# Cross attention by scans and a gated FFN on one core: half gate slots, the weight check summed by TensorE, and residuals over three engines

## The chip, the cores and the metric

The kernel runs on one core of a Trainium2 chip. The metric is the device time of an execution in microseconds (us). The engines are TensorE (PE, with its weight loads as PEld), VectorE (DVE), ScalarE (ACT), GpSimd (POOL) and SyncE (SP), which issues most of the transfers.

## The reference, cut to what matters

Input x is [16, 128, 256], ctx (the values v) the same. One layer: an exponentially decaying average over the 128 time steps (the "wkv" recurrence) with keys layernorm(x), then a feed-forward part of 704 hidden channels.

```python
k = _layernorm(x)
# per channel, over t:   y_t = (sum_{s<t} e^{-(t-1-s)w + k_s} v_s + e^{u+k_t} v_t) / (the same without v)
x = x + wkv(time_decay, time_first, k, ctx_2048)
n = _layernorm(x)
g = einsum('th,ih->ti', n, gate_w) * gate_s
u = einsum('th,ih->ti', n, up_w) * up_s
x = x + einsum('ti,hi->th', silu(g) * u, down_w) * down_s
```

gate_w, up_w and down_w hold only -1, 0 and 1.

## The kernel before

**Tiling.** The 16 sequences are 8 units of two (`UB`), and two units are a group (`GU`) of 512 tokens (`GT`). The first part runs by unit `u`, the FFN by group `g`. The 704 hidden channels are five full tiles of 128 and a rest of 64, six tiles a group (`MC`), numbered on as `n = 6 g + m` (0 to 23).

**A unit's steps.** VectorE makes the statistics of x (`stats1`, `aggr1`), ScalarE the reciprocal deviation (`rstd1`), GpSimd the bias (`bias1`, for units from 2 on in pairs: u = 3, 5, 7), ScalarE the exponentials (`expk`). GpSimd multiplies v by them (`weigh`, units 0 to 3) or VectorE does (`mulp`, units 4 to 7). TensorE transposes both (`e_T`, `p_T`), VectorE runs the recurrences as scans (`scan_e`, `scan_p`) and combines them (`denom`, `numer`), ScalarE makes the reciprocal as log and exponential (`log_den`, `recip`), GpSimd multiplies (`divide`) and adds to x in the channel layout (`first`, `add_y`, buffer `xc`). Then TensorE transposes back (`x1_T`), VectorE makes statistics (`stats2`, `aggr2`), `rstd2` the factors, ScalarE normalises (`norm2`), TensorE transposes (`n_T`), and the result is split into a rounded part and a remainder: `high_n` on ScalarE (`xh`), `low_n` on VectorE (`xl`).

**A group's FFN.** `gate(n)` and `up(n)` are four matmuls of 512 columns each (two halves of the channels, xh and xl), into one of three PSUM slots (`ps_f`, `RING`), taken in turn. `silu(n)` on ScalarE reads the gate's slot, `gated(n)` on VectorE the up's slot and writes `h`. `high_h` (ScalarE) rounds h to `hh`, `low_h` (GpSimd) subtracts to `hl`, and `down(n)` accumulates four matmuls into `ps_d`. The rest tile n = 5, 11, 17, 23 has gate and up in one slot, and `low_rest` on VectorE in place of `low_h`. After six tiles `finish(g)` on VectorE scales `ps_d` and adds it to `xc` in two passes, and SyncE stores each pass. The last tiles of the last group are split into `down` and `downb` by output half.

**The weight check.** Weights come as float32, are copied to a rounded type by GpSimd (`whi`, four equal quarters of the gate and up weights in layout order, then two halves of the down weights). ScalarE sums the low halves of their words (`wcheck`), VectorE compares the three sums with 0 (`wany_`), TensorE adds over the partitions (`count`), VectorE copies the number to `flag` (`publish`), and TensorE reads it and branches to `rest_of_program`, on the rounded weights or the exact ones.

**Order.** Each engine's order is written out by hand in its block. `warm(k)` is k products of the identity with itself, into a slot not yet in use; there are 45 in the opening and 5 in `rest_of_program`. ScalarE switches table sets by `tables(...)`: the exponential and logarithm are in one, silu in another. SyncE's output loop goes by group and half:

```python
for g in range(GROUPS):
    for c in range(CC):
        sp.wait_ge(s_fin, CC * g + c + 1)
        sp.dma_start(out_ch[...], xc[:, c, ...]).then_inc(s_out, 16)
```

Of the kernel before, what the change touches and what calls it, by code (L numbers as in the profile page):

```python
# [5 lines left out]
ALU = mybir.AluOpType  # L6
# [7 lines left out]
P = 128  # L14
# [16 lines left out]
RING = 3  # L31
TAIL = 3 * MC + 2
# [20 lines left out]
def build(nc, x_tok, x_ch, v_tok, v_ch, w_gu, w_d, vecs, out_ch):  # L53
    with ExitStack() as ctx:
# [6 lines left out]
        def sem(name):  # L61
# [16 lines left out]
        mhalf = sb("mhalf", [P, UB])  # L78
# [9 lines left out]
        wany = sb("wany", [P, CC + 1])  # L88
# [31 lines left out]
        hx = sb("hx", [P, GT], F32R)  # L120

# [28 lines left out]
        s_gate, s_up, s_sil, s_h, s_hh, s_hl, s_hx, s_dn, s_fin = (sem(n) for n in (  # L150
            "s_gate", "s_up", "s_sil", "s_h", "s_hh", "s_hl", "s_hx", "s_dn", "s_fin"))
# [52 lines left out]
        def _(sp):  # L204
# [31 lines left out]
        def _(pool):  # L236
# [45 lines left out]
            def rstd2(u):  # L282
# [3 lines left out]
                else:  # L286
# [3 lines left out]
                    nc.gpsimd.tensor_tensor(rs2[:, seqs(u)], ve2[:, seqs(u)], mhalf[:, :], ALU.pow).then_inc(s_rs2, 1)  # L290
# [24 lines left out]

            bias1(0); weigh(0); bias1(1); bias1(3); weigh(1); divide(0); whi(0); first(0); add_y(0); divide(1)
            add_y(1); weigh(2); rstd2(0); whi(1); whi(2); rstd2(1); bias1(5); whi(4); weigh(3); whi(3); divide(2)
            first(1); add_y(2); whi(5); divide(3); rstd2(2); low_h(0); low_h(1); add_y(3); low_h(2); low_h(3)
            rstd2(3); bias1(7); first(2); divide(4); add_y(4); low_h(4); rstd2(4); divide(5); add_y(5); low_h(6)
            low_h(7); rstd2(5); low_h(8); low_h(9); first(3); divide(6); add_y(6); low_h(10); rstd2(6); divide(7)  # L320
            add_y(7); low_h(12); low_h(13); rstd2(7); low_h(14); low_h(15); low_h(16); low_h(18); low_h(19); low_h(20)
            low_h(21); low_h(22)

        @block.scalar
        def _(act):
# [17 lines left out]
            def rstd1(u):  # L343
# [6 lines left out]
                act.wait_ge(s_lv1, k)  # L350
# [72 lines left out]
            def high_h(n):  # L423
# [4 lines left out]
                if m < FULL:  # L428
                    nc.scalar.activation(hh[:, m, :], h[:, n % HS, :], ACT.Copy).then_inc(s_hh, 1)  # L429
                else:  # L430
                    nc.scalar.activation(hx[REST:P, :], h[REST:P, n % HS, :], ACT.Copy).then_inc(s_hh, 1)

            rstd1(0); elift_(); expk(0); rstd1(1); expk(1); rstd1(3); log_den(0); recip(0); expk(2); wcheck(0)
            wcheck(1); log_den(1); recip(1); wcheck(2); expk(3); log_den(2); rstd2a(0); rstd1(5); recip(2); rstd2a(1)
            norm2(0); norm2(1); high_n(0); expk(4); high_n(1); expk(5); log_den(3); recip(3); tables(SILU); silu(0)
            silu(1); high_h(0); silu(2); norm2(2); high_h(1); silu(3); high_h(2); high_n(2); high_h(3); silu(4)
            silu(5); tables(LN_EXP); log_den(4); rstd1(7); recip(4); norm2(3); expk(6); high_n(3); high_h(4)
            high_h(5); log_den(5); expk(7); recip(5); tables(SILU); silu(6); silu(7); norm2(4); high_h(6); silu(8)
            high_n(4); tables(LN_EXP); log_den(6); high_h(7); recip(6); tables(SILU); silu(9); high_h(8); norm2(5)
            high_h(9); silu(10); silu(11); high_n(5); high_h(10); tables(LN_EXP); log_den(7); high_h(11); recip(7)  # L440
            tables(SILU); silu(12); silu(13); norm2(6); high_h(12); high_n(6); silu(14); high_h(13); silu(15)
            high_h(14); silu(16); norm2(7); high_h(15); high_h(16); high_n(7); silu(17); silu(18); high_h(17)
            high_h(18); silu(19); silu(20); high_h(19); silu(21); high_h(20); high_h(21); silu(22); silu(23)
            high_h(22); high_h(23)

        @block.vector
        def _(dve):
# [22 lines left out]
            def wany_():  # L470
# [313 lines left out]
```

## Time and profile before

| | |
|---|---|
| time, median of 3 runs | 105.62 us (105.26 to 105.83) |
| profiled execution, its own time | 105.38 us |
| its span, first to last instruction | 103.6 us |
| busy: TensorE | 93.5 us (90%) |
| busy: VectorE | 80.9 us (78%) |
| busy: ScalarE | 78.1 us (75%) |
| busy: GpSimd | 67.4 us (65%) |
| HBM read, written | 8.55 MB, 2.10 MB |

Busy shares are averages over stages with different limits: the opening to about 28 us, the FFN with the later units beside it, the FFN alone from about 79 us, and the stores at the end. The mean granted TensorE clock was 0.98 of the full one.

### The profile page before, as it was taken

The page shows a single profiled execution, that of the slowest core. Times are in us where ns is not written, and L with a number is a line of the kernel's source. Part 1 is how long each engine was busy: PE and PEld are TensorE (multiplying, and loading weights), DVE is VectorE, ACT ScalarE, POOL GpSimd, SP SyncE. Part 2 cuts the span into 40 slices and gives each one's busy share as a digit, 9 for nine tenths or more (in the row PEclk, how much of TensorE's full clock was granted, in tenths as well). Part 3 has the DMA queues.
Part 4 walks back from the last instruction along what each step waited for, and adds up shares of the span by engine and source line. Part 5 has one row for each costly group of instructions (what it writes and reads, how often), then busy time and mean ns, then how long its engine had stood idle before and what let it go on. Part 6 is the DMA issues. An engine that isn't in the chain of part 4 may idle for free.

```text
span 103.6 us, 1646 instructions
## 1 busy us (share of the span) xinstructions
PE 93.5 (90%) x482; PEld 75.8 (73%) x482; DVE 80.9 (78%) x170; ACT 78.1 (75%) x136; POOL 67.4 (65%) x96
## 2 busy tenths in 40 slices
PE   3997988766999999999999999999999999999930
PEld 3987977644988888668788787858888888888610
DVE  1879999999998999999998998997843544543650
ACT  4355999989995799999999999997858443655400
POOL 2016686999986799894990889869888404364500
PEclk9999999997699999999999999999999999999998
DMA  2999999998000000000005000000500000500005
GB/s 43 301 364 380 406 360 375 377 376 310 23 0 0 0 3 6 0 0 0 0 0 203 0 0 0 9 0 0 203 0 0 0 0 3 193 16 0 0 27 188
DMA packets 6475, 10.78 MB, mean 104 GB/s; under 512 B 576, under 2 KB 3648, under 8 KB 6336
## 3 DMA queue, kind: packets, MB, share of 16 engines
q1 hardware_dynamic: 6320, 10.62, 28.8%
q8 instruction: 6, 0.10, 0.4%
q10 hardware_dynamic: 144, 0.03, 0.3%
q14 instruction: 5, 0.04, 0.1%
HBM read 8.55 MB, written 2.10 MB: 103 GB/s over the span
## 4 chain that ended last, share of the span: by engine, by line
PE 67%; DVE 13%; ACT 7%; DMA 4%; issue 3%; DVEq 1%; SPq 1%
PE ps_f L671 39%; PE ps_d L687 17%; DMA xt<-x_tok 4%; DVE sbe L506 3%; ACT nt L387 3%; PE ps_x L653 3%; PE ps_x L645 2%; DVE st L481 2%; DVE sbp L517 2%; PE ps_f L698 2%; DVE den L531 2%; PE ps_a L626 1%; PE ps_b L635 1%; ACT rden L372 1%; DVE num L541 1%
## 5 line engine op out<-in xcount | busy, mean ns | idle before, releaser
L671 PE MATMUL ps_f<-xh,wgu_r 128*128 128x512 f32 x88 | 36.1, 410 | 0.0
L313 POOL TENSOR_TENSOR hl<-h,hh 128x512 fp32r<-128x512 f32 x20 | 25.7, 1292 | 14.0 <-ACT hh L429 13.9
L671 PE MATMUL ps_f<-xl,wgu_r 128*128 128x512 f32 x88 | 34.8, 396 | 0.0
L578 DVE SCALAR_TENSOR_TENSOR h<-ps_f,vec,sil 128x512 f32<-128x512 f32 (+1 forms) x24 | 17.9, 747 | 11.4 <-PE ps_f L671 7.2
L671 PEld LDWEIGHTS ps_f<-xh,wgu_r 128*128 128x128 f32 x88 | 16.6, 188 | 4.6 <-ACT sil L418 0.7
L671 PEld LDWEIGHTS ps_f<-xl,wgu_r 128*128 128x128 f32 x88 | 16.6, 188 | 3.3
L418 ACT ACTIVATE sil<-ps_f,vec 128x512 f32<-128x512 f32 x20 | 13.5, 687 | 6.8 <-PE ps_f L671 6.7
L698 PE MATMUL ps_f<-ident 128*128 128x128 f32 x100 | 15.8, 320 | 1.6 <-POOL ident L241 1.6
L687 PE MATMUL ps_d<-hh,wd_r 128*128 128x512 f32 x40 | 16.3, 407 | 0.0
L698 PEld LDWEIGHTS ps_f<-ident 128*128 128x128 f32 x100 | 14.9, 234 | 1.6 <-POOL ident L241 1.6
L687 PE MATMUL ps_d<-hl,wd_r 128*128 128x512 f32 x40 | 15.8, 394 | 0.0
L429 ACT ACTIVATE hh<-h 128x512 fp32r<-128x512 f32 x20 | 12.6, 629 | 2.8 <-DVE h L578 2.8
L327 ACT ACT_TABLE_LOAD x8 | 10.3, 1283 | 1.3 <-PEq L778 1.2
L272 POOL TENSOR_TENSOR yk<-num,rden 128x508 f32<-128x508 f32 x8 | 10.3, 1282 | 1.4 <-ACT rden L372 0.8
L278 POOL TENSOR_TENSOR xc<-xc,yk 128x508 f32<-128x508 f32 x8 | 10.2, 1280 | 0.7
L517 DVE TENSOR_TENSOR_SCAN sbp<-decay,ps_b 128x512 f32<-128x512 f32 x8 | 9.7, 1213 | 0.1
L358 ACT ACTIVATE ek<-xt,nb,rs 128x256 f32<-128x256 f32 x16 | 8.7, 590 | 1.4 <-POOL nb L250 1.4
L506 DVE TENSOR_TENSOR_SCAN sbe<-decay,ps_a 128x512 f32<-128x512 f32 x8 | 9.6, 1204 | 0.0
L687 PEld LDWEIGHTS ps_d<-hh,wd_r 128*128 128x128 f32 x40 | 7.5, 188 | 2.1 <-POOL hl L313 0.4
L687 PEld LDWEIGHTS ps_d<-hl,wd_r 128*128 128x128 f32 x40 | 7.5, 188 | 1.6
L387 ACT ACTIVATE nt<-ps_x,nb,rs 128x256 f32<-128x256 f32 x14 | 7.1, 560 | 0.4 <-POOL nb L294 0.3
L531 DVE SCALAR_TENSOR_TENSOR den<-ps_a,fcol,sbe 128x254 f32<-128x254 f32 x16 | 6.9, 474 | 0.0
(73 smaller groups left out, 133.1 us busy)
## 6 DMA issues: line engine op xcount, KB each, us to landing
xt<-x_tok SPq DMA_DIRECT2D x8, 256.0 KB, 7.6
xc<-x_ch SPq DMA_DIRECT2D x4, 512.0 KB, 10.8
out_ch<-xc SPq DMA_DIRECT2D x8, 256.0 KB, 2.5
wgu<-w_gu SPq DMA_DIRECT2D x1, 1408.0 KB, 8.3
vc<-v_ch SPq DMA_DIRECT2D x2, 512.0 KB, 10.5
wd<-w_d SPq DMA_DIRECT2D x1, 768.0 KB, 9.7
vt<-v_tok SPq DMA_DIRECT2D x2, 256.0 KB, 4.9
vt<-v_tok SPq DMA_DIRECT2D x1, 512.0 KB, 11.4
```

The costliest lines, as they stand in the source:

```text
L272: nc.gpsimd.tensor_tensor(yk[:, u % 2, :, 1:T], num[:, u % 2, :, 1:T], rden[:, u % 2, :, 1:T], ALU.mult).then_inc(s_y, 1)
L313: nc.gpsimd.tensor_tensor(hl[:, m, :], h[:, n % HS, :], hh[:, m, :].bitcast(F32), ALU.subtract).then_inc(s_hl, 1)
L327: nc.scalar.preload_act_table_set(name)
L387: last = nc.scalar.activation(nt[:, u % 2, b, :], x1_bank(u)[:, b * C:(b + 1) * C], ACT.Identity, scale=rs2[:, q:q + 1], bias=nb2[:, q:q + 1])
L418: nc.scalar.activation(sil[:, n % 2, :], f, ACT.Silu, scale=vec[:, V_GS + m:V_GS + m + 1]).then_inc(s_sil, 1)
L429: nc.scalar.activation(hh[:, m, :], h[:, n % HS, :], ACT.Copy).then_inc(s_hh, 1)
L506: nc.vector.tensor_tensor_scan(sbe[:, u % 2, :, :].rearrange("p q t -> p (q t)"), decay[:, :, :].rearrange("p q t -> p (q t)"), ps_a[:, :, ...
L517: nc.vector.tensor_tensor_scan(sbp[:, u % 2, :, :].rearrange("p q t -> p (q t)"), decay[:, :, :].rearrange("p q t -> p (q t)"), ps_b[:, :, ...
L578: nc.vector.scalar_tensor_tensor(h[r, n % HS, :], ps_f[r, slot(n, 1) % RING, :], vec[r, V_US + m:V_US + m + 1], sil[r, n % 2, :], ALU.mult ...
L671: last = nc.tensor.matmul(ps_f[:, i % RING, :], w, a, start=c == 0 and x is xh, stop=c == CC - 1 and x is xl)
L687: last = nc.tensor.matmul(ps_d[:, c, :], wd_r[:, m, cs] if exact else wd[:, m, cs], a if exact else a.bitcast(F32), start=m == 0 and i == ...
L698: nc.tensor.matmul(ps_f[:, RING - 1, 0:P], ident[:, :], ident[:, :], start=True, stop=True)
```

## The change

1. **Half gate slots** (`HALVED = 3`): the first three products, gate(0), up(0) and gate(1), are each made in two halves of 256 columns: `gatea` and `upa` for unit 0, as soon as its xl is there (`s_xl` 1), and the other half for unit 1 later.
2. **Check**: `wany_` is gone; `count` sums the three sums themselves, and `publish` compares that number with 0.
3. **Weight copies by tile**: gate and up tiles are interleaved in memory, and `whi` copies three tiles at a time (`PIECE`); a product waits only for its own tiles, `down` for its half of the down weights.
4. **Two residuals elsewhere** (`FIN_ACT = (0, 1)`): for groups 0 and 1 ScalarE scales `ps_d` into a buffer (`settle`, two passes) and GpSimd adds it to `xc` (`add_res`, one instruction). SyncE waits for `s_res` there.
5. **No identity products.**
6. `high_h` of tiles 7, 10, 13 and the reciprocal deviations `rs1` for units 5 and 7 (with their pairs) go from ScalarE to GpSimd; the rest tile's gated value stays in its PSUM slot, which is free only after `low_rest`.
7. **New orders** on the four engines. ScalarE loads tables six times in place of eight.

The diff, cut:

```diff
+HALVED = 3
+PIECE = 3
+HIGH_POOL = (7, 10, 13)
+FIN_ACT = (0, 1)
+RSTD_POOL = (5, 7)
...
+            if k == 2 * FULL:
+                eng.wait_ge(s_hx, g + 1)
+            elif k % 2 == 0:
                 eng.wait_ge(s_sil, n + 1)
...
             for g in range(GROUPS):
                 for c in range(CC):
-                    sp.wait_ge(s_fin, CC * g + c + 1)
+                    if g in FIN_ACT:
+                        sp.wait_ge(s_res, FIN_ACT.index(g) + 1)
+                    else:
+                        sp.wait_ge(s_fin, CC * (g - len([i for i in FIN_ACT if i < g])) + c + 1)
...
+                if u in RSTD_POOL:
+                    i = RSTD_POOL.index(u) + 1
+                    pool.wait_ge(s_mv1, u + 1)
+                    nc.gpsimd.tensor_scalar(lv1[:, q], mv1[:, q, 1], 1.0, EPS, ALU.mult, ALU.add).then_inc(s_ve1, 1)
+                    pool.wait_ge(s_ve1, i)
+                    nc.gpsimd.tensor_tensor(rs1[:, q], lv1[:, q], mhalf[:, :], ALU.pow).then_inc(s_rs1p, 1)
+                    pool.wait_ge(s_rs1p, i)
...
+            def high_h(n):
+                g, m = divmod(n, MC)
+                pool.wait_ge(s_h, n + 1)
+                if g >= 1:
+                    pool.wait_ge(s_dn, CC * (n - MC + 1))
+                nc.gpsimd.tensor_copy(hh[:, m, :], h[:, n % HS, :]).then_inc(s_hhp, 1)
+
+            def add_res(g):
+
+                pool.wait_ge(s_x1, GU * (g + 1))
+                pool.wait_ge(s_set, CC * (FIN_ACT.index(g) + 1))
+                ts = slice(g * GT, (g + 1) * GT)
+                nc.gpsimd.tensor_tensor(xc[:, :, ts], xc[:, :, ts], dsc[:, FIN_ACT.index(g) % 2, :, :], ALU.add).then_inc(s_res, 1)
...
-            bias1(0); weigh(0); bias1(1); bias1(3); weigh(1); divide(0); whi(0); first(0); add_y(0); divide(1)
-            add_y(1); weigh(2); rstd2(0); whi(1); whi(2); rstd2(1); bias1(5); whi(4); weigh(3); whi(3); divide(2)
-            first(1); add_y(2); whi(5); divide(3); rstd2(2); low_h(0); low_h(1); add_y(3); low_h(2); low_h(3)
-            rstd2(3); bias1(7); first(2); divide(4); add_y(4); low_h(4); rstd2(4); divide(5); add_y(5); low_h(6)
-            low_h(7); rstd2(5); low_h(8); low_h(9); first(3); divide(6); add_y(6); low_h(10); rstd2(6); divide(7)
-            add_y(7); low_h(12); low_h(13); rstd2(7); low_h(14); low_h(15); low_h(16); low_h(18); low_h(19); low_h(20)
-            low_h(21); low_h(22)
+            bias1(0); weigh(0); bias1(1); bias1(3); weigh(1); whi(0); divide(0); whi(1); first(0); add_y(0); divide(1)
+            add_y(1); weigh(2); rstd2(0); first(1); weigh(3); rstd2(1); bias1(5); divide(2); add_y(2); whi(2); whi(4)
+            whi(5); whi(3); rstd2(2); divide(3); add_y(3); first(2); low_h(0); low_h(1); low_h(2); low_h(3); rstd2(3)
+            bias1(7); low_h(4); first(3); divide(4); add_y(4); divide(5); rstd2(4); add_y(5); high_h(7); low_h(6)
+            low_h(7); low_h(8); low_h(9); rstd2(5); high_h(10); low_h(10); divide(6); add_y(6); rstd2(6); divide(7)
+            high_h(13); add_y(7); low_h(12); low_h(13); rstd2(7); low_h(14); low_h(15); low_h(16); add_res(0)
+            low_h(18); low_h(19); low_h(20); low_h(21); low_h(22); add_res(1)
...
+            def settle(g):
+
+                k = FIN_ACT.index(g)
+                if k >= 2:
+                    act.wait_ge(s_res, k - 1)
+                for c in range(CC):
+                    act.wait_ge(s_dn, CC * (MC * (g + 1) - 1) + c + 1)
+                    nc.scalar.activation(dsc[:, k % 2, c, :], ps_d[:, c, :], ACT.Copy, scale=vec[:, V_DS + c:V_DS + c + 1]).then_inc(s_set, 1)
+
+            rstd1(0); expk(0); rstd1(1); expk(1); elift_(); rstd1(3); log_den(0); expk(2); recip(0); expk(3)
+            log_den(1); wcheck(0); recip(1); wcheck(1); wcheck(2); rstd2a(0); log_den(2); recip(2); rstd2a(1)
+            norm2(0); norm2(1); high_n(0); expk(4); high_n(1); log_den(3); recip(3); tables(SILU); silu(0); silu(1)
+            high_h(0); norm2(2); silu(2); high_h(1); silu(3); high_n(2); high_h(2); high_h(3); silu(4); silu(5)
+            tables(LN_EXP); log_den(4); expk(5); recip(4); norm2(3); high_h(4); high_h(5); high_n(3); expk(6); expk(7)
+            log_den(5); recip(5); tables(SILU); silu(6); silu(7); settle(0); high_h(6); norm2(4); silu(8); high_n(4)
...
-                dve.wait_ge(s_wsum, CC + 1)
-                nc.vector.tensor_scalar(wany[:, :], wsum[:, :], 0.0, None, ALU.is_gt).then_inc(s_wany, 1)
...
-                nc.vector.tensor_copy(flag[:, :], ps_d[0:1, 1, 0:1]).then_inc(s_flag, 1)
+                nc.vector.tensor_scalar(flag[:, :], ps_d[0:1, 1, 0:1], 0.0, None, ALU.is_gt).then_inc(s_flag, 1)
...
-                if m == 0 and part == 0:
+                if half == 0:
+                    pe.wait_ge(s_xl, 1)
+                elif m == 0 and part == 0:
                     pe.wait_ge(s_xl, GU * (g + 1))
-                if n == 0 and part == 0:
-                    pe.wait_ge(s_wgur, 4)
+                tile = 2 * m + part
+                if g == 0:
+                    pe.wait_ge(s_wgur, tile // PIECE + 1)
                 wait_slot_free(pe, i)
...
+                n_T(0); n_T(1); p_T(3); gatea(0); upa(0); gatea(1); x1_T(2); gate(0); gate(1); e_T(4); up(0); up(1)
+                up(2); gate(2); gate(3); n_T(2); up(3); gate(4); gate(5); x1_T(3); up(4); down(0); down(1); down(2)
+                e_T(5); down(3); n_T(3); down(4); gate(6); up(6); e_T(6); x1_T(4); gate(7); down(5); up(7); gate(8)
...
-            warm(12); e_T(0); warm(3); p_T(0); warm(4); e_T(1); warm(9); p_T(1); e_T(2); warm(8); x1_T(0); warm(9)
+            e_T(0); p_T(0); e_T(1); p_T(1); e_T(2); x1_T(0)
             x1_T(1); e_T(3); count(); p_T(2)
```

## Rows read from the trace of the kernel before

**Rows 1.** The page, shares of the chain that ended last, by engine.
```profile
PE 67%; DVE 13%; ACT 7%; DMA 4%; issue 3%; DVEq 1%; SPq 1%
```
**Rows 2.** Chain of waits in order of time: start us, us, what.
```profile
30.90 0.44 PE ps_x L645 x4
31.34 5.61 PE ps_f L671 x24
...
69.49 2.14 PE ps_f L671 x8
...
97.70 1.45 PE ps_d L687 x5
```
**Rows 3.** Timeline and groups of TensorE: start us, us, what; busy, mean ns.
```profile
1.57 5.49 PE L698 MATMUL ps_f<-ident 128*128 128x128 f32 x24 [1.57 <-POOL ident L241]
...
24.07 0.84 PE L653 MATMUL ps_x<-ident,nt 128*128 128x128 f32 x4 [1.70 <-ACT nt L387]
...
28.77 0.48 PE L671 MATMUL ps_f<-xh,wgu_r 128*128 128x512 f32 x1
...
L698 PE MATMUL ps_f<-ident 128*128 128x128 f32 x100 | 15.8, 320 | 1.6 <-POOL ident L241 1.6
```
**Rows 4.** The end: timelines, windows (last columns PEclk, DMA share, GB/s), SyncE's stores.
```profile
96.35 1.30 POOL L313 TENSOR_TENSOR hl<-h,hh 128x512 fp32r<-128x512 f32 x1 [1.99 <-ACT hh L429]
...
99.23 1.41 DVE L590 SCALAR_TENSOR_TENSOR xc<-ps_d,vec,xc 128x512 f32<-128x512 f32 x2 [1.05 <-PE ps_d L687]
...
100.50:101.00 0.50, 0.00 (x0) 0.00 (x0) 0.15 (x1) 0.00 (x0) 0.00 (x0) 1.00 0.28 106
101.00:101.50 0.50, 0.00 (x0) 0.00 (x0) 0.00 (x0) 0.00 (x0) 0.00 (x0) 1.00 1.03 381
...
102.00:102.50 0.50, 0.00 (x0) 0.00 (x0) 0.00 (x0) 0.00 (x0) 0.00 (x0) 1.00 0.49 172
...
L231 SPq DMA_DIRECT2D out_ch<-xc x2: 332/332/332, 100.0 to 100.7; - x2
...
DMA to landing us min/median/max: 2.3/2.4/2.5
```
**Rows 5.** Windows in the opening: busy of PE, PEld, DVE, ACT, POOL, then PEclk.
```profile
26.00:27.00 1.00, 1.00 (x6) 1.00 (x6) 1.00 (x3) 1.00 (x4) 1.00 (x2) 0.50 0.09 35
...
28.00:29.00 1.00, 1.00 (x11) 1.00 (x10) 0.97 (x2) 0.97 (x2) 0.86 (x3) 1.00 0.00 0
```
**Rows 6.** Timelines of VectorE and GpSimd around the check.
```profile
19.26 1.19 DVE L472 TENSOR_SCALAR wany<-wsum 128x3 f32<-128x3 f32 x1
...
22.08 0.13 DVE L476 CAST flag<-ps_d 1x1 int32<-1x1 f32 x1
...
19.16 1.26 POOL L278 TENSOR_TENSOR xc<-xc,yk 128x508 f32<-128x508 f32 x1
```
**Rows 7.** SyncE's second load of x_ch: issue, and time to landing.
```profile
12.10 0.57 SPq L220 DMA_DIRECT2D xc<-x_ch  x1
...
DMA to landing us min/median/max: 10.5/10.5/10.5
```
**Rows 8.** Timeline of ScalarE in the first half of the FFN.
```profile
30.67 0.69 ACT L418 ACTIVATE sil<-ps_f,vec 128x512 f32<-128x512 f32 x1
...
39.30 0.68 ACT L420 ACTIVATE sil<-ps_f,vec 64x512 f32<-64x512 f32 x1 [0.19 <-PE ps_f L671]
40.01 1.28 ACT L327 ACT_TABLE_LOAD   x1
...
43.06 1.02 ACT L387 ACTIVATE nt<-ps_x,nb,rs 128x256 f32<-128x256 f32 x2
43.98 1.09 ACT L358 ACTIVATE ek<-xt,nb,rs 128x256 f32<-128x256 f32 x2
```
**Rows 9.** Groups of GpSimd by shape: busy us, mean ns, idle before.
```profile
L313 POOL TENSOR_TENSOR hl<-h,hh 128x512 fp32r<-128x512 f32 x20 | 25.7, 1292 | 14.0 <-ACT hh L429 13.9
...
L290 POOL TENSOR_TENSOR rs<-ve,mhalf 128x2 f32<-128x2 f32 x6 | 4.2, 702 | 0.5
...
L265 POOL TENSOR_TENSOR xc<-xc,vec 128x8 f32<-128x8 f32 x4 | 0.9, 215 | 0.1
```

More of the change, by code:

```diff
@@ L430, in high_h @@
                 else:
[L431 to L441, printed above, removed]
@@ L446, in _ @@
+            high_h(20); silu(22); high_h(21); silu(23); high_h(22); high_h(23)
         @block.vector
@@ L603, in finish_c @@
                 residual(GROUPS - 1, c)
-            lift_(); stats1(0); aggr1(0); stats1(1); stats1(2); decay_(); stats1(3); aggr1(1); aggr1(2); scan_e(0)
-            aggr1(3); denom(0); scan_p(0); scan_e(1); numer(0); denom(1); scan_p(1); scan_e(2); numer(1); denom(2)
-            stats2(0); stats1(4); wany_(); aggr2(0); stats1(5); aggr1(4); aggr1(5); stats2(1); publish(); aggr2(1)
-            scan_p(2); stats1(6); scan_e(3); numer(2); low_n(0); denom(3); low_n(1); scan_p(3); stats1(7); numer(3)
@@ L614, in _ @@
-            numer(7); gated(12); gated(13); finish(1); low_n(6); gated(14); stats2(7); aggr2(7); gated(15); gated(16)
-            low_n(7); gated(17); gated(18); low_rest(17); gated(19); finish(2); gated(20); gated(21); gated(22)
-            gated(23); low_rest(23); finish_c(0); finish_c(1)
+            lift_(); stats1(0); aggr1(0); stats1(1); stats1(2); decay_(); aggr1(1); aggr1(2); stats1(3); scan_e(0)
+            aggr1(3); denom(0); scan_p(0); scan_e(1); numer(0); denom(1); scan_p(1); numer(1); scan_e(2); denom(2)
@@ new lines, in _ @@
+            stats2(0); stats1(4); aggr2(0); stats1(5); stats2(1); publish(); aggr2(1); aggr1(4); scan_p(2); aggr1(5)
+            numer(2); scan_e(3); low_n(0); denom(3); low_n(1); scan_p(3); stats2(2); numer(3); aggr2(2); gated(0)
+            stats1(6); gated(1); scan_e(4); aggr1(6); gated(2); stats1(7); gated(3); low_n(2); mulp(4); denom(4)
+            stats2(3); gated(4); aggr2(3); gated(5); scan_p(4); aggr1(7); numer(4); scan_e(5); mulp(5); low_n(3)
+            denom(5); scan_p(5); low_rest(5); numer(5); stats2(4); aggr2(4); gated(6); mulp(6); gated(7); scan_e(6)
@@ L618, in _ @@
+            denom(6); gated(8); low_n(4); gated(9); scan_p(6); stats2(5); aggr2(5); numer(6); gated(10); gated(11)
+            scan_e(7); mulp(7); low_n(5); denom(7); low_rest(11); scan_p(7); stats2(6); aggr2(6); gated(12); numer(7)
+            gated(13); gated(14); low_n(6); stats2(7); aggr2(7); gated(15); gated(16); gated(17); low_n(7)
+            low_rest(17); gated(18); finish(2); gated(19); gated(20); gated(21); gated(22); gated(23); low_rest(23)
+            finish_c(0); finish_c(1)
         @block.tensor
@@ L693, in down_ @@
                         last.then_inc(s_tail[c], 1)
[L695 to L698 removed]
             def count():
                 pe.wait_ge(s_ones, 1)
[L702 removed]
+                pe.wait_ge(s_wsum, CC + 1)
                 for k in range(CC + 1):
[L704 removed]
+                    last = nc.tensor.matmul(ps_d[0:1, 1, 0:1], ones[:, :], wsum[:, k:k + 1], start=k == 0, stop=k == CC)
                 last.then_inc(s_wcnt, 1)
```

118 lines of the change are left out of this document (62 added, 56 removed).

## The prediction

> **What bounds the kernel now.** I read the chain of waits first, then TensorE's timeline, then the last five microseconds. The chain runs over TensorE for 67% of the span [rows 1]. From the first gate product at 28.77 to the last down product at 99.15 [rows 2, 3] TensorE stands still only for moments. Its work there: 264 products of 512 columns at 5.61/24 = 0.234 us [rows 2] are 61.7 us, and fifteen groups of four transposes (x1_T and n_T of units 2 to 7, e_T of units 5 to 7) at 0.44 us [rows 2] are 6.6 us, together 68.3 of the 70.4 us. So about 2.1 us of stalls are all that a better order can win behind the first product; the other thing to win is an earlier start. What ends the span is different again: the last subtraction on GpSimd (low_h(22)) ends at 97.65, VectorE's two residuals run from 99.23 to 100.64, SyncE issues a store after each, at 100.0 and 100.7, and the second lands 2.5 us after its issue [rows 4]. Behind 97.65 lie 5.95 us of the 103.6 us span. The profiled execution took 105.38 us, 0.24 under the median of 105.62, and 1.78 lie outside its span; my sum goes from 105.38.
>
> **The opening.** Removed are 50 identity products (the 100 records of 0.32 us [rows 3]; each runs as two), which filled pauses. They are off the path, but they are the cover for the clock. The first 24 records took 5.49 us, 0.229 each, where at full clock a group of four transposes of the same size takes 0.44 or 0.11 each [rows 2, 3]: the start ran at half rate. After the one long pause the clock was granted at half (26 to 27 us: 0.50, that is 1.2 of 2.4 GHz) and was full again from 28 us [rows 5]. Without the fillers TensorE is mostly idle until 24 us, so I count the transposes at half clock, 0.88 us a group. Each of the early groups then gives its result 0.4 us later; on VectorE the scans of e(1) and p(1) slip by 0.3 to 0.7 us, but numer(1) now stands before scan_e(2), so divide(1) begins about 0.3 us earlier than before. The Trainium skill (TensorE: Matmul & The Clock Gate, section "What's actually happening") says that the idle state is the half clock and that activity releases it; by it the early transposes and the first products are slow, which the row of 26 us bears out, and it speaks against this part.
>
> The check: the comparison wany took 1.19 us for three elements, from 19.26 to 20.45, while GpSimd's add over 508 elements ran from 19.16 to 20.42; the copy of the flag out of PSUM took 0.13 us though GpSimd was busy too [rows 6]. So 1.19 is not the price of a comparison, and the new publish, a comparison that reads PSUM, I take at 0.15 us (upper bound 1.19). The Trainium skill (SBUF — State Buffer, "Who interferes with whom") says that VectorE and GpSimd share a port pair that one locks for its whole instruction, and that an instruction with one input in PSUM does not need it; by it publish costs 0.13 to 0.15, while by the bare row of the comparison it would cost 1.19 and move everything behind it by 1.0. The removed wany gives nothing of its 1.19 on the path, because VectorE then only waits for x1_T(1), which follows add_y(1) at about 20.1 (20.42 before).
>
> With one unit later weight sums and count() behind e_T(3), the flag comes at 22.5 (22.21 before [rows 6]) and n_T(0) at 24.3 (24.07 [rows 3]). On GpSimd first(1) now stands before weigh(3) and rstd2(1), and it waits for the second load of x_ch: issued at 12.10 and landing 10.5 us later, at 22.6 [rows 7]. Its queue would have been there at 21.95, so weigh(3), then rstd2(1) slip by 0.7, norm2(1) and n_T(1) come at 24.7 and 25.8, p_T(3) at 26.7, and the first half product at about 27.6, 1.2 us before 28.77. The twelve half matmuls for the unit 0 halves are 1.5 to 2.6 us (full or half clock), and need no low_n(1). A matmul of 256 columns is not in the trace: it costs at least half of 0.234 and at most all of it; a straight line from the 0.11 of a transpose of 128 columns to 0.234 gives 0.15, and I take 0.13, between that and the half: 0.3 us more for the 24 of them (bounds 0 and 2.8). But e_T(4), 0.44 us, which lay before 28.77, now lies behind. And silu(0), which frees the first slot, comes at 30.7 as before (30.67 [rows 8]): one expk less before it, but denom(3) later. Net: up(1) starts some 0.4 us earlier, and 1 us later if the clock stays at half until 31 us.
>
> **The middle.** silu(5) follows gate(5): 38.9 for 39.30. Then comes ScalarE's chain: the table load of 1.28, log_den(4), recip(4), norm2(3). expk(5) (1.09) is now in it where rstd1(7) was (half of that as an estimate), so of the 0.4 nothing is left: norm2(3) at 43.3 for 43.06 [rows 8]. high_h(4) follows at 44.3. On GpSimd bias1(7) now holds its own power (0.70 [rows 9] and three small ones, 1.5 us in all) and waits for aggr1(7), now behind scan_p(4), so low_h(4) runs from 44.95 to 46.2. down(4) stands in front of gate(6) in the new order, so TensorE, there at 44.8, waits some 1.4 us. At up(7) it is then about 0.3 us behind the old one. After that the lighter ScalarE pays: two of eight table loads go (2.57 us), three high_h and two rstd1 go to GpSimd, and two settles come, 1.3 us each as two passes like a silu's 0.69 [rows 8]; VectorE loses four residual passes at 0.7 [rows 4]. The old stalls between 64 and 69.5 us, where the chain shows up(13) at 69.49 [rows 2], go; I get up(13) at 69.0, 0.5 ahead. What the moved work costs where it goes lies in gaps: high_h on GpSimd 0.6 each and add_res(0) 2.4, against 14.0 us in which it waited for ScalarE's hh [rows 9]. From 69.5 TensorE was saturated, so 0.5 us of lead lasts, and the last subtraction, low_h(22), ends at 97.2 instead of 97.65.
>
> **The tail.** Here is the step that decides. add_res(1) stands behind low_h(22) in GpSimd's order. SyncE stores the groups in order, and its loop waits for add_res(1) before both stores of group 1; the stores of groups 2 and 3 are queued behind it. So six stores, of which before only two were left, go out after it. Its cost: 1.29 us for 512 elements and 0.215 for 8 give 2.14 ns an element, so 1,024 elements take 0.215 + 1,016 x 0.00214 = 2.4 us (at most two of 1.29, 2.6) [rows 9]. So: 97.2 + 0.1 + 2.4 = 99.7 for the first issue. Before, data began to move about 0.85 us after the issue (106 GB/s over the half microsecond before 101.0 are 53 KB, 0.14 us at full rate), flowed at 381 GB/s, ended near 102.25 (172 GB/s in the last half microsecond) and landed 0.9 us later [rows 4]. Six stores of 262 KB are 1.57 MB, at 381 GB/s 4.1 us; the issues themselves take 0.33 us each, which is faster. Last landing: 99.7 + 0.85 + 4.1 + 0.9 = 105.5, where before it was 100.7 + 2.5 = 103.2. That is 2.35 us more. If the six stores moved no faster than they are issued or much of it overlapped, the floor is two stores behind a late issue, 99.7 + 0.66 + 2.5 = 102.9, which would hide it all; the order of the queue excludes that. What goes is the stores' cover: before, the stores of group 1 and 2 lay beside the products of the next group.
>
> The sum: 105.38 + 2.35 (tail, with the 0.45 us of lead already taken off) = 107.7.
>
> **The rivals.** (a) The tail as above, stream within 1.2 us of my reckoning: 106.5 to 108.9, likeliest 107.7; chance 0.65. (b) Stream later still, by the clock: with few matmuls in the pauses it stays at half until some 31 us; 3.4 us of products at half clock lose 1.7, and nothing later has that much slack: low_h(22) at 98.7, 109.2. For it speaks 0.50 at 26 us [rows 5]; against it that n_T(1), p_T(3) and the half products now follow each other closely. Chance 0.17. By the Trainium skill's section on the clock gate, cited above, this is the case that its rule leads to. (c) The other side: the stream runs without stalls. One mechanism: silu, high_h and low_h come early enough because of the head start and the two table loads saved, so the waits at 44.8 and 64 to 69.5 don't exist. Then low_h(22) ends at 27.6 + 68.3 + 0.4 + 0.3 - 1.5 (what follows it) = 95.1, and the time is 107.7 - 2.1 = 105.6: no change. It decides from 2.3 us of lead over the old 97.65 on (108.15 - 2.3 = 105.9, within 0.5%); for a gain of over 0.5% it needs 3.3, which asks for an earlier start as well. Against it stands expk(5) in the chain to norm2(3). Chance 0.12. (d) The tail's transfers are cheaper, as if GpSimd reached add_res(1) before silu(23) had let high_h(22) go: the order forbids it; some smaller cut, 106.2, 0.06.
>
> **How the numbers follow.** 107.7 is (a). 0.5% (0.53 us) is what a measurement of this kernel can tell from no change. The range takes (a) whole, the better half of (b), and of the rest what is above 106.1: 106.1 to 109.2. Case (a)'s own range is 106.5 to 108.9. Slower: (a), (b), and half of (d), with something of (c)'s upper end: 0.87; same: most of (c) and half of (d): 0.09; faster: 0.04, if the start is earlier than 27 us as well.
>
> **What would show it.** In the new profile: SyncE's stores of groups 1, 2 and 3 all issued after GpSimd's 2.4 us addition, later than TensorE's last product; DMA at some 380 GB/s over 4 of the last 6 us; TensorE's end near 98.7; GpSimd waiting for the x_ch load near 22 us; the clock at half until 28 us; a wait of TensorE for GpSimd's hl near 45 us; six table loads. I am wrong if the group 1 addition ends before 97 us, or if the products start before 27 us and TensorE ends before 97 us.

## The result, and the profile after

The changed kernel takes 112.05 us (median of six runs, 110.38 to 112.33), the one before 105.42 (104.94 to 105.83): 1.057 times as long, interval 1.051 to 1.063. I had forecast slower and 107.7 us, range 106.1 to 109.2. The direction was right and the size much too small: 6.6 us were lost, where I had 2.3.

The profiled execution of the changed kernel took 111.83 us, its span is 110.0. Its page, part 1 and two rows of part 2 (forty slices of 2.75 us):

```profile
PE 84.0 (76%) x394; PEld 66.4 (60%) x394; DVE 78.1 (71%) x165; ACT 75.8 (69%) x131; POOL 75.7 (69%) x105
...
PEclk9999999999999999976999999999999999999985
...
GB/s 58 291 380 422 389 319 377 367 385 124 3 6 0 3 0 0 0 0 0 0 0 0 6 0 0 3 0 0 0 0 6 0 191 0 3 0 6 171 340 68
```

Two places stand out. The granted clock dips in the 18th and 19th slices (47 to 52 us), where before it had dipped only in the opening. And the last three slices carry stores, at 340 GB/s in the last but one, where before only the last two did.

The opening came as worked out. TensorE's timeline (start, duration, instruction, in brackets the idle time before it and what ended it), and then one row each of VectorE's, ScalarE's and GpSimd's, beside [rows 3, 6, 8]:

```profile
24.38 1.11 PE L705 MATMUL ps_x<-ident,nt 128*128 128x128 f32 x4 [0.95 <-ACT nt L434]
...
27.49 0.49 PE L727 MATMUL ps_f<-xh,wgu_r 128*128 128x256 f32 x1 [0.23 <-DVE xl L615]
27.82 0.28 PE L727 MATMUL ps_f<-xl,wgu_r 128*128 128x256 f32 x1
27.94 0.28 PE L727 MATMUL ps_f<-xh,wgu_r 128*128 128x256 f32 x1
```
```profile
22.42 0.15 DVE L527 TENSOR_SCALAR flag<-ps_d 1x1 int32<-1x1 f32 x1 [0.26 <-PE ps_d L756]
```
```profile
31.19 1.26 ACT L465 ACTIVATE sil<-ps_f,vec 128x512 f32<-128x512 f32 x2
```
```profile
21.94 0.21 POOL L298 TENSOR_TENSOR xc<-xc,vec 128x8 f32<-128x8 f32 x1
```

n_T(0) starts at 24.38 (24.3 forecast), the first half product at 27.49 (27.6), and a half matmul starts every 0.12 us (0.13). The four transposes of n_T(1) take 1.11 us; n_T(0) took 0.84 in the old kernel. The flag's comparison costs 0.15. silu(0) starts at 31.19, 0.5 us behind the old 30.67.

The middle did not. TensorE's timeline around down(4), GpSimd's, and then windows of the trace (length, then busy us and instructions begun of PE, PEld, DVE, ACT and POOL, then PEclk, DMA share and GB/s):

```profile
47.55 0.47 PE L744 MATMUL ps_d<-hh,wd_r 128*128 128x512 f32 x1 [2.10 <-POOL hl L346]
47.85 0.40 PE L744 MATMUL ps_d<-hl,wd_r 128*128 128x512 f32 x1
...
49.69 0.63 PE L727 MATMUL ps_f<-xh,wgu_r 128*128 128x512 f32 x1
50.12 0.63 PE L727 MATMUL ps_f<-xl,wgu_r 128*128 128x512 f32 x1
```
```profile
44.21 0.19 POOL L275 TENSOR_SCALAR lv<-mv 128x4 f32<-128x4 f32 x1 [0.66 <-DVE mv L538]
44.48 1.01 POOL L277 TENSOR_TENSOR rs<-lv,mhalf 128x4 f32<-128x4 f32 x1
...
46.13 1.27 POOL L346 TENSOR_TENSOR hl<-h,hh 128x512 fp32r<-128x512 f32 x1
```
```profile
46.00:47.00 1.00, 0.00 (x0) 0.00 (x0) 0.97 (x3) 1.00 (x3) 0.92 (x2) 1.00 0.00 0
...
48.00:49.00 1.00, 1.00 (x5) 0.74 (x4) 1.00 (x2) 1.00 (x2) 0.92 (x2) 0.61 0.00 0
49.00:50.00 1.00, 1.00 (x4) 0.81 (x3) 0.97 (x2) 0.95 (x3) 1.00 (x1) 0.50 0.00 0
50.00:51.00 1.00, 1.00 (x4) 0.71 (x4) 0.91 (x3) 1.00 (x1) 0.16 (x1) 0.50 0.00 0
```

TensorE stands still for 2.10 us in front of down(4), until GpSimd's low_h(4), which began at 46.13 behind bias1(7) with its power of 1.01 us. Then the products run at half clock (granted 0.50 of 2.4 GHz, that is 1.2 GHz): the starts at 49.69 and 50.12 are 0.43 us apart where they were 0.234 [rows 2].

The tail: GpSimd's timeline, then SyncE's last six stores (ns of one issue, first and last issue) with their times to landing, then windows, beside [rows 4]:

```profile
98.71 1.30 POOL L346 TENSOR_TENSOR hl<-h,hh 128x512 fp32r<-128x512 f32 x1 [1.47 <-ACT hh L476]
99.97 2.39 POOL L361 TENSOR_TENSOR xc<-xc,dsc 128x1024 f32<-128x1024 f32 x1
```
```profile
L256 SPq DMA_DIRECT2D out_ch<-xc x6: 333/450/1027, 102.4 to 104.8; - x6
DMA to landing us min/median/max: 2.5/3.3/4.7
```
```profile
103.50:104.00 0.50, 0.00 (x0) 0.00 (x0) 0.00 (x0) 0.00 (x0) 0.00 (x0) 1.00 1.01 373
...
106.50:107.00 0.50, 0.00 (x0) 0.00 (x0) 0.00 (x0) 0.00 (x0) 0.00 (x0) 0.50 1.02 258
107.00:107.50 0.50, 0.00 (x0) 0.00 (x0) 0.00 (x0) 0.00 (x0) 0.00 (x0) 0.50 0.95 311
107.50:108.00 0.50, 0.00 (x0) 0.00 (x0) 0.00 (x0) 0.00 (x0) 0.00 (x0) 0.50 0.37 139
...
108.50:109.00 0.50, 0.00 (x0) 0.00 (x0) 0.00 (x0) 0.00 (x0) 0.00 (x0) 0.50 0.07 29
```

All six stores leave behind the addition of 2.39 us. Behind the last subtraction (ends at 100.01) lie 10.0 us, before 5.95. So the span's 6.4 us are 2.4 of a later last subtraction (100.01 for 97.65) and 4.0 of a longer tail.

### The profile page after: what moved, and what is told of

It reads as the page before. It is cut to its first block, busy times and chain, and to the rows that moved or that the text cites. A ratio compares the mean times of both kernels' runs of the same rounds, so it can differ in the third digit from the quotient of the medians.

```text
span 110.0 us, 1479 instructions
## 1 busy us (share of the span) xinstructions
PE 84.0 (76%) x394; PEld 66.4 (60%) x394; DVE 78.1 (71%) x165; ACT 75.8 (69%) x131; POOL 75.7 (69%) x105
## 4 chain that ended last, share of the span: by engine, by line
PE 54%; POOL 17%; DVE 9%; issue 6%; ACT 4%; DMA 2%; DVEq 1%; POOLq 0%; ACTq 0%
PE ps_f L727 35%; PE ps_d L744 9%; POOL yk L305 5%; POOL xc L311 5%; POOL hl L346 4%; PE ps_a L678 4%; PE ps_x L697 3%; DVE sbp L568 2%; DVE sbe L557 2%; DMA vec<-vecs 2%; POOL rs L277 2%; PE ps_x L705 2%; ACT L374 1%; DVEq L59 1%; PE ps_d L697 1%
## 5 line engine op out<-in xcount | busy, mean ns | idle before, releaser
L727 PE MATMUL ps_f<-xh,wgu_r 128*128 128x512 f32 (+1 forms) x94 | 37.3, 401 | 0.3 <-DVE xl L615 0.2
L727 PE MATMUL ps_f<-xl,wgu_r 128*128 128x512 f32 (+1 forms) x94 | 35.9, 386 | 0.0
L727 PEld LDWEIGHTS ps_f<-xh,wgu_r 128*128 128x128 f32 x94 | 18.3, 195 | 5.0 <-DVE xl L615 0.6
L630 DVE SCALAR_TENSOR_TENSOR h<-ps_f,vec,sil 128x512 f32<-128x512 f32 x20 | 15.0, 748 | 8.5 <-PE ps_f L727 6.0
L727 PEld LDWEIGHTS ps_f<-xl,wgu_r 128*128 128x128 f32 x94 | 18.3, 195 | 3.1
L678 PE MATMUL ps_a<-ident,ek 128*128 128x128 f32 x32 | 6.7, 348 | 8.2 <-ACT ek L405 7.2
L476 ACT ACTIVATE hh<-h 128x512 fp32r<-128x512 f32 x17 | 10.6, 629 | 1.4 <-DVE h L630 1.2
L678 PEld LDWEIGHTS ps_a<-ident,ek 128*128 128x128 f32 x32 | 5.1, 181 | 9.0 <-issue 7.2
L599 DVE BATCH_NORM_STATS2 st<-ps_x 128x6 f32<-128x256 f32 x14 | 5.3, 419 | 3.1 <-PE ps_x L697 3.1
```

Source lines behind the costliest of these rows:

```text
L630: nc.vector.scalar_tensor_tensor(h[:, n % HS, :] if m < FULL else up, up, vec[r, V_US + m:V_US + m + 1], sil[r, n % 2, :], ALU.mult, ALU.m ...
L678: last = nc.tensor.transpose(ps_a[:, c * UB + b, :], ek[:, u * UB + b, c * P:(c + 1) * P], ident[:, :])
L727: last = nc.tensor.matmul(ps_f[:, i % RING, ts], w, a, start=c == 0 and x is xh, stop=c == CC - 1 and x is xl)
```

## The experiments

**The changed kernel, one cost at a time.** Add the two residuals of GpSimd together, early:

```diff
-low_h(16); add_res(0)
-low_h(18); ...; low_h(22); add_res(1)
+low_h(16); add_res(0); add_res(1)
+low_h(18); ...; low_h(22)
```

> The changed kernel with add_res(1) directly behind add_res(0) in GpSimd's order, where GpSimd stood idle for 4.3 us; nothing else differs. Theory 'the queued stores cost the tail': the profiled changed kernel has 10.0 us behind its last subtraction, the old one 5.95, so 4.0 us are saved, 107.9 us where the changed one takes 111.9; SyncE then stores group 1 near 90 us and only two stores remain at the end. Rival 'the products end late, the tail only adds what the later end brings': under 1 us is saved. TensorE's end stays near 101.5 in both.

Measured: 106.93 us (106.32 to 108.35), 1.018 (1.008 to 1.028) times the kernel before. Three of its four runs took 106.3 to 107.0 at a mean clock of 1.00, one 108.35 at 0.984. Against 112.05 that is 5.1 us less, more than the 4.0 of the tail: in this profile the clock stayed full behind down(4), though TensorE waited for it just as long. The windows of the two kernels from 44.8 to 54 us, the changed one first, then this one; behind them this one's TensorE row of down(4), its last two stores, and GpSimd's group of the additions:

```profile
44.80:54.00 9.20, 7.10 (x30) 5.67 (x30) 6.97 (x14) 6.93 (x12) 6.32 (x8) 0.81 0.00 0
```
```profile
44.80:54.00 9.20, 7.08 (x38) 5.74 (x37) 8.53 (x17) 8.52 (x15) 7.58 (x11) 1.00 0.00 0
```
```profile
47.69 0.47 PE L744 MATMUL ps_d<-hh,wd_r 128*128 128x512 f32 x1 [2.12 <-POOL hl L346]
```
```profile
L256 SPq DMA_DIRECT2D out_ch<-xc x2: 332/332/332, 101.0 to 101.6; - x2
```
```profile
84.01 4.80 POOL L361 TENSOR_TENSOR xc<-xc,dsc 128x1024 f32<-128x1024 f32 x2
```

In the same 9.2 us and the same busy time TensorE began 38 matmuls at full clock, and 30 where the mean granted clock was 0.81. The last subtraction ends at 98.59 and the span at 104.5: a tail of 5.9 us, the old one's. The tail's 4.0 us are shown, and the rival, under 1 us, is out. So the wait does not always bring the clock down. The changed kernel's own runs point the same way: five took 111.8 to 112.3 at a mean clock of 0.967 to 0.972, and one 110.38 at 0.981. Only one of the six was profiled, so for the others it is the mean that says whether the clock fell in the middle.

The opening of this run shows something else. Its first half products start 0.21 us apart (TensorE's timeline), where those of the changed kernel's profile were 0.12 apart:

```profile
28.05 0.41 PE L727 MATMUL ps_f<-xh,wgu_r 128*128 128x256 f32 x1
28.27 0.41 PE L727 MATMUL ps_f<-xl,wgu_r 128*128 128x256 f32 x1
```

They reach full rate only from about 29.7 us on. Yet down(4) comes at 47.69 against 47.55, so the rate of the first products hardly moves it here.

**Fill the wait.**

```diff
+def fill(k):
+    pe.wait_ge(s_sil, 5)
+    warm(k)
...
-e_T(5); down(3); n_T(3); down(4)
+e_T(5); down(3); n_T(3); fill(9); down(4)
```

> The changed kernel with nine identity products (18 records of 0.11 us, 2.0 us) between n_T(3) and down(4), where TensorE stood idle for 2.1 us and the clock was granted at half from 48.2 to 51.6 us. Theory 'the clock falls by the wait': the wait itself stays, down(4) begins at 47.5 as before, the clock stays full, and 1.7 us are won, 110.2 us. Rival 'the wait costs, the clock doesn't, since the other engines set the pace there': no change, 111.9.

Measured: 110.71 us (110.45 to 110.98), four runs, all at 0.981 to 0.983: near the 110.38 of the changed kernel's one run with the higher clock, and now each time. TensorE's timeline (each fp32 identity product is two records, so nine are x18):

```profile
45.58 2.17 PE L755 MATMUL ps_f<-ident 128*128 128x128 f32 x18
47.85 0.47 PE L744 MATMUL ps_d<-hh,wd_r 128*128 128x512 f32 x1
48.17 0.39 PE L744 MATMUL ps_d<-hl,wd_r 128*128 128x512 f32 x1
```

down(4) starts no earlier, and the products behind it are at full clock. 112.05 - 110.71 = 1.3 us is what the clock's fall costs in the medians, and 1.45 us lie between the profiled 111.83 and the 110.38. In the profiles, from the start of down(4) to the end of the last subtraction, it is 52.46 us (47.55 to 100.01) against 50.88 here (47.85 to 98.73): 1.6 us. In five profiles with filled waits (this one, and four further on) the clock is full behind down(4); in four with an unfilled wait of 2.1 us it fell in two.

**Both.** 

> Both edits of the two runs before: add_res(1) early, and nine identity products in the wait in front of down(4). If the two costs are separate, their gains add: 4.0 and 1.7 us, 106.2 us, within 1% of the old kernel's 105.4. If the tail's cost hangs on the products' late end, the sum is smaller.

Measured: 107.0 us (106.39 to 108.85), 1.010 (1.000 to 1.020). The tail's gain is there (110.7 to 107.0), and the filler adds nothing to the early additions, whose clock had stayed full in most runs without it: 107.0 and 106.9. I had expected 106.2, taking both costs as certain. One of its four runs took 108.85 at a mean clock of 0.986, against 0.991 to 1.00 of the others; where its clock fell isn't recorded, so a filled wait is no proof of a full clock throughout. What remains to the 105.64 of the kernel before is 1.4 us, in neither the tail nor, in most runs, the middle's clock.

**The stores alone, in the kernel before.**

```diff
 for g in range(GROUPS):
+    if g == 1:
+        sp.wait_ge(s_hl, FULL * GROUPS)
```

> The kernel before, but SyncE holds the stores of groups 1 to 3 until GpSimd's last subtraction, low_h(22), is done (97.65 in the old profile). Nothing else is changed. Theory 'queued stores': six stores leave from 97.7 on; with the 7.1 us that six took in the changed kernel from first issue to last landing the last lands at 104.8 instead of 103.2, so 1.6 us slower, 107.0, less what the last two wait for their residuals. By the sum of the prediction (0.85 + 4.1 + 0.9 = 5.85 us) it would be 103.55 and the kernel 0.4 us slower.

Measured: 106.69 us (106.58 to 107.59), 1.014 (1.005 to 1.022), so 1.05 us slower: between the two sums. Its last six stores:

```profile
L233 SPq DMA_DIRECT2D out_ch<-xc x6: 333/442/1239, 97.3 to 101.0; - x6
DMA to landing us min/median/max: 2.5/3.4/3.9
```

The last store was issued at 101.0 and landed 3.6 us later, where before it took 2.5. So held stores cost 1.05 us when they may start at 97.3, while the last products and residuals still run. In the changed kernel they start at 102.4, behind the 2.4 us addition, and with nothing left beside them.

**The wait made shorter.** On top of the early additions:

```diff
-rstd2(3); bias1(7); low_h(4)
+rstd2(3); low_h(4); bias1(7)
```

> On top of the run with add_res(1) early (106.9 us, down(4) at 47.69 after 2.1 us of idle TensorE): in GpSimd's order low_h(4) goes in front of bias1(7), which waited for aggr1(7) and took 1.9 us with its power. Theory 'bias1(7) in front of low_h(4) makes the wait': low_h(4) starts with high_h(4)'s end near 45.3, down(4) 0.9 us earlier, at 46.8, and expk(6) 1.3 us later. Rival 'low_n(3) is as late': gate(6) behind down(4) needs it at 47.4, and 46.8 plus 0.9 is later than that, so the 0.9 us are kept at gate(6); what follows loses by the later expk(6), net 0 to 0.9 us faster than 106.9.

Measured: 108.5 us (107.96 to 109.61), 1.6 us slower than with bias1(7) in front. The profile is of its slowest run, 109.61. There down(4) came at 46.99 in place of 47.69, as expected, but expk(6) waited for bias1(7) until 48.88, ScalarE's table load slid from 49.97 to 52.34 and silu(6) from 51.27 to 53.6. So ScalarE's queue in front of silu(6), not the wait for low_h(4), paces what follows, and my expectation that the net would not be a loss was wrong.

With low_h(4) still in front, rstd1(7) back on ScalarE, and two more exchanges:

```diff
-RSTD_POOL = (5, 7)
+RSTD_POOL = (5,)
...
-norm2(3); high_h(4); high_h(5); high_n(3); expk(6)
+norm2(3); high_h(4); rstd1(7); high_n(3); high_h(5); expk(6)
...
-scan_e(5); mulp(5); low_n(3)
+scan_e(5); low_n(3); mulp(5)
```

> On top of the run with add_res(1) early, four steps around the wait for down(4): low_h(4) in front of bias1(7) on GpSimd; rstd1(7) back on ScalarE behind high_h(4), so that bias1(7) is two instructions again; high_n(3) in front of high_h(5); low_n(3) in front of mulp(5). Theory 'this wait is the rest of the difference': down(4) near 46.8, gate(6) near 47.7, expk(6) within 0.8 us of where it was; 1 to 1.3 us faster than 106.9, level with the old kernel. Rival 'the loss lies elsewhere, in the work shifted to GpSimd later on': under 0.3 us.

Measured: 106.82 us (106.41 to 107.31). down(4) came 0.9 us earlier (46.81), silu(6) 0.7 us later (51.97), and silu(8) at 55.69 where it had been at 55.67. Nothing is gained: the rival's number, but not for the rival's reason, which was work shifted to GpSimd later on.

**The opening.** On top of the early additions, the 45 identity products of the old kernel's opening are put back:

```diff
-e_T(0); p_T(0); e_T(1); p_T(1); e_T(2); x1_T(0)
+warm(12); e_T(0); warm(3); p_T(0); warm(4); e_T(1); warm(9); p_T(1); e_T(2); warm(8); x1_T(0); warm(9)
```

> On top of the run with add_res(1) early: the 45 identity products of the opening are back between the same transposes as in the old kernel. Theory 'the removed fillers cost the clock': the early transposes take 0.44 instead of 0.88 us a group, scan_p(1) comes 0.9 us earlier; but what follows waits for GpSimd's divide and add_y, so n_T(0) comes 0.3 us earlier, the first half product 0.3 to 0.7 us, and the whole 0 to 0.5 us, since ScalarE's silu(0) starts at 31.2 for other reasons. Rival 'the fillers are worth their whole difference in clock': over 1 us faster. Second rival: fillers delay the transposes behind them, 0 to 0.5 us slower.

Measured: 107.38 us (106.65 to 108.0), 1.018 (1.010 to 1.026). Here the time misleads. down(4) came at 46.44, 1.25 us earlier than without, but all four runs were at 0.951 to 0.984, and in the profile the granted clock is 0.50 from 47 to 50 us, and silu(7) follows silu(6) by 2.8 us, as in the changed kernel: the clock fell in the middle. So both were put together, with nine fillers in the wait as well:

> add_res(1) early, the 45 fillers of the opening back, and nine fillers in the wait in front of down(4). In the run with the opening's fillers alone down(4) came at 46.44 in place of 47.69, but the clock then fell in the middle and took it back. Theory 'the opening's fillers are worth 1.2 us and the middle's keep them': the clock stays full, 105.6 us, level with the old kernel (105.5). Rival 'the fillers of the opening change nothing that lasts': 106.8, as without them.

Measured: 105.27 us (median of ten runs, 104.96 to 106.49), 0.996 (0.993 to 1.000) times the kernel before, so level with it. Against the same kernel without the opening's fillers (107.0) that is 1.7 us. The opening's fillers are worth that in the medians, together with the middle's; alone they showed no gain (107.38 against 106.93).

The run that was profiled is the slowest of the ten, 106.49 at a mean clock of 0.957 (the others 0.984 to 0.996). Here are its clock row (forty slices of 2.62 us) and two rows of TensorE's timeline:

```profile
PEclk9999999995559999999999999999999999999995
```
```profile
27.38 0.41 PE L727 MATMUL ps_f<-xh,wgu_r 128*128 128x256 f32 x1
27.59 0.41 PE L727 MATMUL ps_f<-xl,wgu_r 128*128 128x256 f32 x1
```

In spite of the fillers the clock is at half from 24.1 to 30.9 us, behind the 1.50 us in which TensorE waited for n_T(0); down(4) comes at 47.91, and this run has nothing of the gain. So the fillers do not always keep the opening's clock, and no profile shows this kernel as its median run has it.

The same part alone, in the kernel before, with the 45 products taken out:

> The kernel before, with the 45 identity products of the opening taken out and nothing else (the five near the first product stay). One part of the change alone. Theory 'the fillers buy the opening's clock': the transposes at half clock move the opening by 0.9 to 1.3 us, and the first products run at half until some 28 to 31 us, 1.0 to 2.5 us slower than 105.5. Rival 'they are off the path': within 0.3 us, or faster, since no transpose waits behind a filler.

Measured: 107.22 us (106.78 to 108.14), 1.019 (1.012 to 1.025): by the ratio 2.0 us hang on the fillers, by the medians of this comparison (105.72 before) 1.5. silu(0) went from 30.67 to 32.35. In the profile the early groups of transposes take 1.1 us where they took 0.66, which moves the chain that depends on them, while the first products start 0.23 us apart, at full clock.

**The halves.** On top of the early additions, the first three products whole again, e_T(4) in front of them:

```diff
-HALVED = 3
+HALVED = 0
...
-p_T(3); gatea(0); upa(0); gatea(1); x1_T(2); gate(0); gate(1); e_T(4); up(0); up(1)
+p_T(3); e_T(4); gate(0); x1_T(2); gate(1); up(0); up(1)
```

> On top of the run with add_res(1) early: the first three products are whole again, made after low_n(1), with e_T(4) in front of them. Theory 'the halves' lead is lost in the waits that follow': TensorE starts products 1.8 us later, at 29.3, loses 1.0 us at up(1), and of that the idle time near 45 us takes up a part, 0 to 1 us slower than 106.9. Rival 'the halves are worth their head start': 1.2 us slower or more.

Measured: 110.0 us (109.73 to 110.28), 1.042 (1.036 to 1.048): 3.1 us slower than with the halves. Its opening and its wait in TensorE's timeline:

```profile
29.49 0.80 PE L727 MATMUL ps_f<-xh,wgu_r 128*128 128x512 f32 x1
30.08 0.63 PE L727 MATMUL ps_f<-xl,wgu_r 128*128 128x512 f32 x1
30.51 0.63 PE L727 MATMUL ps_f<-xh,wgu_r 128*128 128x512 f32 x1
...
49.49 0.47 PE L744 MATMUL ps_d<-hh,wd_r 128*128 128x512 f32 x1 [2.11 <-POOL hl L346]
```

The first products started at half clock, 0.43 us apart, as the transposes before them had run (1.1 us a group). And the 1.8 us by which down(4) came later (49.49 against 47.69) stand behind the same 2.1 us of idle time: that idle time is no slack that absorbs a later start, it moves along with it. The chain that ends in low_h(4) starts at the first products too. Behind it, the last store landed 4.2 us after its issue where the run with the halves had 2.5. The 1.8 and these 1.7 make up the 3.4 us between the two profiled runs. Why the store landed late is open. The run changes e_T(4)'s place together with the halves, and does not tell the two apart.

**Two tries for more.** With the four steps of the shorter wait on top of all fillers:

> The run before with the four steps that shorten the wait for down(4) (low_h(4) in front of bias1(7), rstd1(7) on ScalarE, high_n(3) in front of high_h(5), low_n(3) in front of mulp(5)) and six fillers there in place of nine. Theory 'ScalarE's silu(6) sets the pace behind the wait': as without the fillers nothing is gained by the steps, within 0.4 us of the run before. Rival 'TensorE's wait sets it': 0.8 us faster.

Measured: 105.93 us (104.99 to 108.6, twelve runs), 1.001 (0.997 to 1.004). No gain. Its profile is of the slowest run, 108.6, with the clock at half in the opening from 23.8 to 30.7 us.

The other try builds on that kernel, and takes expk(7) out of the stretch in front of silu(6):

```diff
-high_h(5); expk(6); expk(7)
+high_h(5); expk(6)
...
-norm2(5); recip(6)
+norm2(5); expk(7); recip(6)
...
-down(7); e_T(7); down(8); n_T(5); down(9); down(10)
+down(7); down(8); n_T(5); down(9); down(10); e_T(7)
```

> The run before with expk(7) (1.1 us of ScalarE) moved from in front of silu(6) to behind norm2(5), with e_T(7) behind down(10) on TensorE. Theory 'ScalarE's queue in front of silu(6) holds the ring': silu(6) about 1.0 us earlier, 0.5 to 1.0 us faster than the run before, 104.8 us or less, faster than the old kernel. Rival 'it is given back at the next table load': recip(6) and with it x1_T(6) come 1.1 us later, no gain or up to 0.5 us slower.

Measured: 109.64 us (109.05 to 110.59), 1.042 (1.034 to 1.049). silu(6) did come earlier (50.92, where the profile of the kernel under it had 52.34 and the one with the early additions alone 51.27), but e_T(7), now late on TensorE, stood in front of low_n(5) and denom(7) by way of VectorE's scan_e(7) and mulp(7), and the gate product of the next group (TensorE's timeline) and ScalarE's log (ScalarE's) waited:

```profile
69.05 0.51 PE L727 MATMUL ps_f<-xh,wgu_r 128*128 128x512 f32 x1 [2.70 <-DVE xl L615]
```
```profile
69.81 0.72 ACT L414 ACTIVATE rden<-den,elift 128x508 f32<-128x508 f32 x1 [3.76 <-DVE den L582]
```

The move left VectorE's order unchanged, in which scan_e(7) and mulp(7) stand in front of low_n(5). It says nothing on what expk(7) costs where it was.

## Why the prediction was wrong

**The tail: mechanism right, size short.** add_res(1) took 2.39 us (2.4 forecast), and all six stores left behind it. Their time from first issue to last landing was put at 0.85 + 4.1 + 0.9 = 5.85 us; it was 104.8 + 4.7 - 102.4 = 7.1. The flow was not a steady 381 GB/s: it fell to 258 and 311 in two of the late windows, and small remains of 25 to 29 GB/s followed for 1 us before the last landing. 1.25 us of the miss. Early additions put the tail back to 5.9 us.

**The middle: the step that failed.** It is "TensorE, there at 44.8, waits some 1.4 us", in its time and in its price. TensorE was there at 45.45 (the end of n_T(3)) and waited 2.10 us, until 47.55 instead of 46.2. Of these 1.35 us, 0.76 came in front of bias1(7), which began at 44.21 behind aggr1(7) where 44.95 less 1.5 makes 43.45. Bias1(7) itself took 1.92 in place of 1.5, mostly from the power on four columns, 1.01 us where I used the row for two, 0.70 [rows 9]; and 0.15 lie between the end of low_h(4) and TensorE's start. It is no accident of one run: from the first half product to down(4) I had 18.6 us (27.6 to 46.2), and the four profiles with an unfilled wait of 2.1 us have 20.0 to 20.2 from their first product, also where the first products ran at half clock.

And I priced the wait as a wait alone, with nothing for the clock behind it. The clock's fall, which I had as rival (b), I placed at the first products. In this profile they were at full rate from 27.8 us on, and in the run with early additions only from 29.7, at no cost that reached down(4). It fell at 48 us instead, behind the new wait, from 48.2 to 51.6, and took 1.6 us. Without it the last subtraction would have ended at 98.4, 1.25 us behind my 97.2; with it, at 100.0. These 1.25 us are the lateness of the middle as a whole. The wait for low_h(4) does not make them by itself: with down(4) 0.9 us earlier nothing was won, since silu(6) came later. What it would take to win them is open.

Behind this wait the trace shows 1.2 GHz in place of 2.4. The Trainium skill (TensorE: Matmul & The Clock Gate, "What's actually happening") has the throttled clock as the default state, which activity releases. The direction agrees with this trace; but behind a wait of 2.12 us in the run with early additions the clock stayed full, so the rule alone did not settle a wait of this length, and I should have put the fall into the sum with a chance of its own.

**The sum.** 107.7 + 1.25 (tail) + 1.25 (later middle) + 1.6 (clock) = 111.8; the profiled execution took 111.83.

**The opening: times right, worth wrong.** n_T(0), the first half product and the half matmul's price came within 0.1 us. I set the early start of the half products against the slower transposes and saw a small lead at up(1). The runs show two large terms that nearly cancel: the fillers taken out lose 1.5 to 2.0 us (107.0 against 105.27 in the new kernel, 107.22 against 105.72 in the old), and the halves, with the place of e_T(4), win 1.8 us at down(4). That the transposes would run at half clock was right; what hangs on them I sized too small: silu(0) came at 31.19 where I had 30.7. That GpSimd would wait for the x_ch load near 22 us was wrong: first(1) ran at 21.94 without waiting, since the load landed at about 20.9.

**Rivals.** (c), a stream without stalls, did not come: the waits are there, and even with all fillers and early additions the kernel is at 105.3. (d) did not come. What was right: the new comparison takes 0.15 us out of PSUM, at 22.42, while GpSimd multiplies from 22.10 to 23.37. By the Trainium skill (SBUF — State Buffer, "Who interferes with whom") it needs no shared port, and the row agrees. That the old comparison's 1.19 us was a wait for GpSimd fits with this, but isn't shown: the old one was also larger, 128x3 against 1x1. Table loads are six.

**Where the 6.6 us went.** 4.0 into the tail (early additions), about 1.5 into the middle's clock (filled wait), 1.7 into the opening's clock (opening's fillers). These are 7.2; the rest of the change, the halves, two table loads less and the shifted work, gives back some 0.6 in sum. The version with these three mended is level with the kernel before: 0.996 (0.993 to 1.000).

Open: whether the wait of 2.1 us brings the clock down varies from run to run, and no run here shows what decides it (filled, it did not fall there in any of the five profiles). The same holds for the opening's clock with its fillers. And it is open why the last store lands 4.0 to 4.4 us after its issue in three profiles, of different kernels, and 2.5 in the others that end with a single pair.

## What to carry to other kernels

Read the in-order queue of stores as part of the critical path: a late producer for an early output holds all outputs behind it, and costs their whole transfer when no work is left beside them. When you work out a wait on TensorE, price it twice: the wait, and, with a chance, the products behind it at half rate. And don't take idle time in front of an instruction for slack before you know that its producer doesn't start at the same place.

## What the runs showed of the hardware

The granted clock in the windows reads 1.00 from 0 to 28 us in the changed kernel, although four transposes took 1.09 to 1.12 us there and 0.60 to 0.66 at full rate later. In the run with early additions it reads 1.00 up to 104 us, although its first half products start 0.21 us apart, and 0.12 from 29.7 us on. So in the opening the matmuls' own spacing has to be read, and a run's mean clock leaves that stretch out.

Behind a wait of 2.1 us in a busy stream the clock fell in five of six runs of one kernel, and in one of four of another that differs only later in the program; for all but the two profiled runs that is read from the mean clock. With identity products in the wait none of five profiles shows a fall there.

Six stores of 262 KB in a row took 7.1 us in two profiles, 1.2 more than their bytes at the rate of a pair; SyncE's own issues stretched from 0.33 to 1.03 us.
